# Swiglu and gated feed-forward of a conditioned block stack: the high half of the product is written by ScalarE instead of VectorE

## The reference, cut to what matters

```python
def _L1_cond_ref(...):
    ...
    h2 = modulate(rmsnorm(x, norm2_w), sh_mlp, sc_mlp)
    ff = jax.nn.silu(h2 @ w1.T) * (h2 @ w3.T) @ w2.T
    x = x + g_mlp * ff

def _L2_cond_ref(...):
    ...
    vg = x @ tg_fc_w.T + tg_fc_b
    v_, g_ = jnp.split(vg, 2, axis=-1)
    x = x + jax.nn.gelu(v_, approximate=False) * jnp.tanh(g_) @ tg_out_w.T + tg_out_b
```

## Time and profile before

| | us |
|---|---|
| median of 3 runs | 2367.48 (2367.0 to 2367.68) |
| the profiled execution | 2364.86 |
| its span, first to last instruction | 2363.1 |
| swiglu stage | 1384 to 1612 |
| gate stage | 2184 to 2324 |
| TensorE busy over the span | 2005.7 (85%) |
| VectorE busy | 1455.1 (62%) |
| ScalarE busy | 968.7 (41%) |
| GpSimd busy | 835.4 (35%) |

### The profile page before, as it was taken

How to read it: one execution, slowest core, us unless ns; L and a number is a source line. 1 busy time by engine, 2 the same in 40 slices (tenths; PEclk the granted TensorE clock), 3 DMA queues, 4 the chain that set the end, 5 groups by cost and what they waited for, 6 DMA issues and landing times. The chain is left out here.

```text
span 2363.1 us, 41380 instructions
## 1 busy us (share of the span) xinstructions
PE 2005.7 (85%) x15274; PEld 1565.9 (66%) x15274; DVE 1455.1 (62%) x2120; ACT 968.7 (41%) x1594; POOL 835.4 (35%) x759
## 2 busy tenths in 40 slices
PE   4829999999999799867787679997877877998998
PEld 4618878878887577646565567774655656777775
DVE  1236655656566455468888856775777774554554
ACT  0024434434444566534454433332333345664332
POOL 0041111211011344456665723345656572443000
PEclk9959999999999999978999989998998999999999
DMA  7120000000000100010000000001000000000001
GB/s 301 55 74 2 2 2 1 1 2 1 1 1 10 49 0 0 0 41 2 0 0 0 1 25 0 0 1 36 1 0 0 0 2 27 0 0 32 5 0 72
DMA packets 19519, 44.28 MB, mean 19 GB/s; under 512 B 3200, under 2 KB 11200, under 8 KB 18176
## 3 DMA queue, kind: packets, MB, share of 16 engines
q1 hardware_dynamic: 19392, 42.48, 5.1%
HBM read 36.18 MB, written 6.29 MB: 18 GB/s over the span
## 5 line engine op out<-in xcount | busy, mean ns | idle before, releaser
L1223 DVE TENSOR_TENSOR Glb<-Gfb,Ghb 128x512 fp32r<-128x512 f32 x176 | 168.2, 964 | 101.6 <-ACT Ghb L1176 100.0
L523 POOL TENSOR_TENSOR Tm<-Dv,MOD 128x512 f32<-128x512 f32 x96 | 111.3, 1179 | 298.6 <-DVE Dv L580 208.0
L633 PE MATMUL bank<-HH,W1b 128*128 128x512 f32 x448 | 183.8, 410 | 13.2 <-PEq L1493 6.9
L633 PE MATMUL O<-Ghb,W2b 128*128 128x512 f32 x352 | 144.1, 409 | 54.0 <-DVE Glb L1223 52.4
L634 PE MATMUL bank<-HL,W1b 128*128 128x512 f32 x448 | 177.2, 396 | 0.0
L635 PE MATMUL bank<-HH,W1b 128*128 128x512 f32 x448 | 176.9, 395 | 0.0
L1378 PE MATMUL bank<-WQKa,HH 128*128 128x512 f32 x256 | 101.4, 483 | 78.3 <-DVE HL L588 63.6
L653 POOL TENSOR_TENSOR spare<-RT 128x1 f32<-128x1 f32 x48 | 9.5, 197 | 446.0 <-DVE RT L644 446.0
L512 POOL TENSOR_TENSOR XS<-Tm 128x512 f32<-128x512 f32 x48 | 70.5, 1469 | 245.6 <-ACT Tm L478 245.6
L635 PE MATMUL O<-Ghb,W2b 128*128 128x512 f32 x352 | 138.4, 393 | 0.0
L634 PE MATMUL O<-Glb,W2b 128*128 128x512 f32 x352 | 137.8, 392 | 0.0
(11 more groups left out here) (244 smaller groups left out, 5470.0 us busy)
## 6 DMA issues: line engine op xcount, KB each, us to landing
w<-l_w_dram SPq DMA_DIRECT2D x4, 2048.0 KB, 26.7
wm<-w_mods_dram SPq DMA_DIRECT2D x6, 768.0 KB, 12.1
X<-xT_dram SPq DMA_DIRECT2D x4, 1024.0 KB, 36.3
out_dram<-XO SPq DMA_DIRECT2D x8, 512.0 KB, 2.7
W2b_f<-l_w_dram SPq DMA_DIRECT2D x11, 256.0 KB, 5.0
WQK_f<-l_wqk_dram SPq DMA_DIRECT2D x8, 256.0 KB, 7.1
W1b_0f<-l_w_dram SPq DMA_DIRECT2D x8, 256.0 KB, 3.5
b2r<-l_b2r_dram SPq DMA_DIRECT2D x1, 1024.0 KB, 7.7
```

Source lines behind the costliest of these rows:

```text
L523: nc.gpsimd.tensor_tensor(Tm[:, k].rearrange("p (b t) -> p b t", t=T), Dv[:, k].rearrange("p (b t) -> p b t", t=T), m, ALU.mult).then_inc( ...
L633: nc.tensor.matmul(out, w_lo_ap, x_hi, start=first, stop=False)
L1223: nc.vector.tensor_tensor(Gl[m % gb][:], gf, Gh[m % gb][:].bitcast(F32), ALU.subtract).then_inc(g_lo.h, 1)
```

## The change

The cast into `Gh` moves from VectorE to ScalarE as an activation of kind Copy, for the swiglu and gate kinds. ScalarE waits for the product (`g_mul`) and for a free `Gh` buffer before it. VectorE keeps its wait for `g_hi`, which ScalarE now signals. `Gh` and `Gl` get three buffers in the swiglu kind and four in the gate kind. In ScalarE's list the copy of tile m stands behind Silu (or Tanh) of tile m and in front of `act_rstd`, `act_hh`, `act_square`, `act_sqh` and `x_act` of that tile.

```diff
-                gb = 4 if kind == "gelu" else 2
+                gb = 3 if kind == "swiglu" else 4
...
                                 if gate:
                                     nc.scalar.activation(Gt[m % 2][:], BK[2 + m % 2][:], ACT.Tanh, bias=bias(1, m)).then_inc(g_act.h, 1)
+                                if kind != "gelu":
+                                    act.wait_ge(g_mul.h, g_mul.at(g + 1))
+                                    act.wait_ge(g_used.h, g_used.at(g - gb + 1))
+                                    nc.scalar.activation(Gh[m % gb][:], Gf[m % 2][:], ACT.Copy).then_inc(g_hi.h, 1)
                                 f, cc, pp = late(fr, nf, c, p, more)
...
                             if kind != "gelu":
-                                dve.wait_ge(g_used.h, g_used.at(g - 1))
-                                nc.vector.tensor_copy(Gh[m % 2][:], gf).then_inc(g_hi.h, 1)
                                 dve.wait_ge(g_hi.h, g_hi.at(g + 1))
                             nc.vector.tensor_tensor(Gl[m % gb][:], gf, Gh[m % gb][:].bitcast(F32), ALU.subtract).then_inc(g_lo.h, 1)
```

## The result

The changed kernel takes 2378.54 us in the median of six runs (2374.57 to 2385.52), the kernel before 2367.42 in six runs beside it (2361.16 to 2373.14). The ratio is 1.0048, with a 95% interval of 1.0027 to 1.0069: slower. The profiled execution took 2378.67 us with a span of 2376.9, 13.8 us more than before.

The account below looks back on a forecast made before the run. TensorE paces both stages, so the cast matters only where the chain product, cast, subtraction ends last. Swiglu loses 7.1 us and gate 1.2, together 8.3: median 2367.48 becomes 2375.8 us, 0.35% slower, range 2369.5 to 2384.

Parts of the forecast that it names:

- The load waits for the copy: ScalarE, swiglu tile 0: the table load of line 487 starts when the copy ends, 1.74 us later in chunk 3.
- The chain of one tile: Product start to subtraction start takes 1.39 us, before 1.18 in swiglu or 1.27 in gate.
- The hand-overs of 0.04 us: VectorE to ScalarE takes 0.04 us by the trace; the same estimated for the way back.
- TensorE at tile 1: Swiglu chunk 3: the subtraction of tile 1 is 0.60 us late, so TensorE waits about 0.5 us.
- The reserve that I took as fixed: Swiglu chunk 3, tile 1: subtraction ends at 1479.23, TensorE starts at 1479.40 without a wait; used up, not overdrawn.
- Tile 2: Swiglu: the subtraction arrives 0.06 us too late and waits for GpSimd's second instruction; 0.14 us gained of 1.2.
- The buffers at nothing: The wait for a free buffer is already met whenever the cast could start, with two or four buffers; no cost.
- The gate stage: 0.12 us more at each of seven borders, 0.2 each at first and last tile; together 1.2 us.
- Chunks 6 and 7: Last swiglu chunks: load 1.81 us later in chunk 6, 1.5 taken for both; 1.35 us each, 2.7 together.
- Clock drops: TensorE's clock falls after two of eight swiglu stalls, 1.7 us lost each; the forecast sum adds no more.
- more clock drops: Rival: TensorE idles at tile 1 too; one to five more drops at 1.7 us give 2377.5 to 2384.3; chance 0.24.
- Faster by a load that passes a waiting activation: Rival: line 487's load starts straight after Silu, tile 1 terms vanish; with port won too, 2359.4 us; chance 0.06.

Follow-up runs that it names:

- before_held_load2: Kernel before, cast on VectorE, but in swiglu tile 0 ScalarE waits for the product and copies one column ahead of the table load; one execution, 2368.44 us.
- preload_first: Changed kernel, but in swiglu tile 0 ScalarE loads the Ln and Exp table ahead of the copy; median 2367.28 us, ratio 0.9999 to the kernel before.
- gpsimd_yields: Changed kernel, but in swiglu chunks 0 to 5 GpSimd waits for tile 2's subtraction between its two line 523 instructions; median 2370.11 us, ratio 1.0010.
- before_again: The kernel before, unchanged, profiled once more; 2367.09 us, swiglu stage 225.12.
- two_buffers: Changed kernel with two buffers of Gh and Gl again in swiglu and gate; one execution, 2372.88 us.
- before_yields: Kernel before, cast on VectorE, but in swiglu chunks 0 to 5 GpSimd waits for tile 2's subtraction between its line 523 instructions; median 2364.43 us, ratio 0.9978.
- preload_yields: Changed kernel with both the table load ahead of the copy and GpSimd's wait between its line 523 instructions; median 2366.29 us, ratio 0.9995.
- before_split_norm: Kernel before, but in all feed-forward stages the normalisation's three small steps run after tile 0, only the product into Dv after tile 1; median 2373.3 us, ratio 1.0021.

## Why the prediction was right, point by point

The time, 2375.8 forecast and 2378.5 measured, lies in the range, and the direction and the mechanism hold. The distance is larger in the profiled execution, 2373.2 forecast and 2378.7 measured: 3.2 us of it are clock drops and 2.6 lie outside the two stages. The steps:

- **The load waits for the copy.** Right, and the main cause. It starts 1.44 us after the product in chunk 3; forecast were 1.35 (0.68 + 0.04 + 0.63). Held alone it costs (before_held_load2), put ahead it gives 8.2 us back (preload_first), more than the 6.9 that the stage had lost without drops.
- **The chain of one tile.** Forecast 1.39 us, measured 1.38 to 1.39, and 1.46 at tile 0 of the loop's chunks (the buffers, below; 1.54 in chunk 0) and in most tiles of chunks 6 and 7. The hand-overs of 0.04 us held at 1.38: in chunk 3, tile 2 of gpsimd_yields the product's 0.68 us end at 1484.20, the copy starts at 1484.23 and the subtraction 0.03 us after the copy ends.
- **TensorE at tile 1.** The wait of about 0.5 us didn't show as such: in chunks 1 to 5 it was 0.17 to 0.22 us (1.38 in chunk 0, 0.72 in chunk 6). The delay is there all the same. In chunk 3 the down projection of tile 1 starts 8.10 us after the product of tile 0 (1479.05 to 1487.15), before 7.53: 0.57 us later, against the 0.5 that I had summed, and chunks 3 and 5 grew by 0.43 and 0.48 against 0.46. TensorE is itself late at tile 1, through the border: in the even chunks it waits 0.98 us for the residual step, against 0.78 before. The reserve that I took as fixed moved along with the shift, so the loss was split over two waits.
- **Tile 2.** Right. The subtraction still lasted 1.50 us, and ended 0.55 us after the second GpSimd instruction (1492.78 and 1493.33). The margin was 0.05 us where I had 0.06: in chunk 3 the second GpSimd instruction started at 1491.74, the subtraction at 1491.83, and so it went in every one of the loop's chunks. By the Trainium skill ("SBUF — State Buffer", section "Who interferes with whom") whichever starts first holds the port pair for its whole instruction; gpsimd_yields agrees, as the subtraction that finds the pair free lasts 0.69 us. The copy, between 629 and 634 ns in 48 cases, agrees with the part on ScalarE. The long cast of before_again doesn't follow from the start times of the rows: it starts at 1607.74, 0.45 us before the first fill, and still ends behind the last.
- **The buffers at nothing.** Nearly. They cost 0.08 to 0.09 us in a chunk, by a register operation of the wait that stands behind the product (two_buffers). I had costed the wait's outcome, not its instructions.
- **The gate stage.** 1.1 us, forecast 1.2, and right by luck: the term was too small, and a clock drop that went made up for it. The waits grew by 2.0 us: most border waits by 0.20 us, the 0.12 of the chain and the 0.08 of the buffers, and the waits at the first and the last tile by 0.33 and 0.28 against 0.2 each. The last down projection without its clock drop gave 0.9 us back.
- **Chunks 6 and 7.** 0.91 and 1.60 us against 1.35 each, an estimate "built alike". The sum (2.5 against 2.7) is right by luck: next to before_again (27.18 us), chunk 7 would have grown by nothing (27.12).
- **Clock drops.** This term of the sum was mis-sized: none more in the forecast, two more in the profiled execution, 3.2 us. In that execution the rival "more clock drops" came true, and without them the swiglu stage grew by 6.9 us against 7.1. How many drops the other executions had isn't known, so I can't divide the 11.1 us between the medians. I also counted eight stalls of about 2 us before; of the eleven waits in rows 1, seven are of 1.7 to 2.1 us, and chunk 7 has none above 0.5.
- **Faster by a load that passes a waiting activation.** Refuted by the chunk 3 rows of after.

The drops go with long waits. The twelve profiled executions have 23 drops in the swiglu stage, and each begins within 1.5 us of the end of a TensorE wait of 1.81 to 2.15 us. 29 waits of 1.8 us or more have none behind them, one of 2.14 us among them. With GpSimd's wait the loop's waits at tile 2 are at most 1.42 us and none has a drop behind it (before_yields has one in chunk 6 behind 1.81 us, preload_yields one in chunk 0 behind 2.15 at tile 0); before_split_norm with waits of up to 1.76 had none. Before had drops at the same two places in both executions, the kernels with the copy at changing ones. What decides between two equal waits stays open.

## What to carry to other kernels

An instruction moved to an idle engine brings its wait along, and everything queued behind it on that engine waits too: list what stands behind it first, table loads above all, and put ahead of it what doesn't need its result (here that gave the whole loss back). Before removing work from an engine, look for what would hold up its next instruction anyway; here a port shared with GpSimd ate the gain. One wait on GpSimd's side gained 0.22%, while the move of 80 casts lost 0.48%. And take stages apart by clock before calling a sum right: two terms here came out only because a clock drop or a blocked cast fell the other way.

## What the runs showed of the hardware

- A table load stands in ScalarE's order behind an activation that waits for a semaphore (1480.49, behind a copy that ended at 1480.47). Its 1.28 us can be put under another engine's work if it is issued ahead of the wait; Copy then ran under the logarithm's table without another load.
- A Copy of 128x512 into fp32r on ScalarE kept to 629 to 634 ns in after, beside busy GpSimd and VectorE, while the same cast on VectorE took 0.43 to 3.19 us.
- A blocked VectorE subtraction ended 0.54 to 0.55 us after GpSimd's instruction ended. One that starts 0.05 us after it, with GpSimd then waiting, takes its normal 0.69 us; with GpSimd going straight on it waited for the whole second instruction.
- A blocked cast that is already waiting when GpSimd goes from one instruction to the next may get in (0.80 us in all) or stay out for four more (2.77 us); its lead on the end of GpSimd's instruction was 0.52 to 0.53 us in both cases.
- A register operation of 0.035 us for a wait's target, standing behind the semaphore that ends last, made the copy start 0.11 us after its product ended instead of 0.03, though the wait itself was met.
- One clock drop cost 1.6 us, eight matmuls at 0.63 us instead of 0.39. All 23 of the swiglu stage stood behind waits of 1.81 to 2.15 us, and 29 waits of 1.8 us or more had none.
